# A mixture-of-experts tail on one Trainium2 core: token rows gathered per expert tile in place of rows scattered into a sorted buffer

## The reference

```python
x = x + attention(layernorm(x), context)
xn = layernorm(x)
probs = softmax(xn @ gate_w.T)
p, idx = top_k(probs, 2)
y_k = gelu(xn @ w1[idx_k].T + b1[idx_k]) @ w2[idx_k].T + b2[idx_k]      # k = 0, 1
out = x + sum over k of p_k * y_k
```

## Time and profile before

| | |
|---|---|
| median of 3 executions | 332.87 us (332.79 to 333.19) |
| profiled execution | 333.22 us |
| its span (first to last record) | 331.5 us |
| PE busy | 258.6 us |
| ACT busy | 231.7 us |
| DVE busy | 172.8 us |
| POOL busy | 79.4 us |
| mean granted clock of PE | 0.925 of 2.4 GHz |

### The profile page before, as it was taken

The page is one execution under the profiler, slowest core; times in us unless marked ns, Lnnn a source line. Parts: engine busy times, 40 slices in busy tenths (PEclk is TensorE's granted clock), DMA queues, the critical chain, the costliest instruction groups (busy, mean ns, idle before and its releaser), DMA issues.

```text
span 331.5 us, 6252 instructions
## 1 busy us (share of the span) xinstructions
PE 258.6 (78%) x1856; PEld 126.5 (38%) x1856; DVE 172.8 (52%) x422; ACT 231.7 (70%) x365; POOL 79.4 (24%) x134
## 2 busy tenths in 40 slices
PE   2689687399999999989899999986474079999940
PEld 2455445112222121212122222225463069898940
DVE  4798944224454535353545354447751327676612
ACT  4358565379999999999999999971794025555520
POOL 8893002100000000000000000402057604444430
PEclk9999965879999999999999999999898559999995
DMA  7999580010101010101010010199501171001114
GB/s 199 373 397 405 191 176 2 17 29 2 36 4 40 0 40 12 28 12 28 16 24 22 18 28 11 36 356 272 70 26 55 48 185 34 31 28 33 34 32 190
DMA packets 28930, 29.29 MB, mean 88 GB/s; under 512 B 15261, under 2 KB 22833, under 8 KB 28784
## 3 DMA queue, kind: packets, MB, share of 16 engines
q1 hardware_dynamic: 27456, 26.21, 26.4%
q0 software_dynamic: 1456, 2.86, 2.9%
HBM read 21.62 MB, written 7.45 MB: 88 GB/s over the span
## 4 chain that ended last, share of the span: by engine, by line
issue 31%; PE 23%; ACT 16%; DVE 11%; POOL 6%; SPq 5%; DMA 4%; ACTq 1%; DVEq 1%; POOLq 1%
ACT w2T L996 8%; ACT arenaB L996 8%; PE bank L1280 7%; PE bank L1401 5%; PE bank L1262 5%; SPq L318 4%; PE bank L1409 3%; POOL qS L380 3%; DVE arenaC L528 2%; DVE arenaB L899 2%; SPq L290 1%; PE bank L1170 1%; DMA arenaA<-ys_dram 1%; DMA x_sb<-in_x_dram 1%; DVE arenaB L905 1%
## 5 line engine op out<-in xcount | busy, mean ns | idle before, releaser
L716 DVE TENSOR_TENSOR arenaA<-bank,arenaA 128x512 f32<-128x512 f32 x80 | 55.2, 690 | 82.7 <-PE bank L1280 82.7
L996 ACT ACTIVATE arenaB<-bank 128x1024 f32<-128x1024 f32 x80 | 77.5, 1022 | 8.5 <-PE bank L1262 6.5
L996 ACT ACTIVATE w2T<-bank 128x1024 f32<-128x1024 f32 x80 | 76.7, 1028 | 3.0 <-PE bank L1262 1.7
L1262 PE MATMUL bank<-qS,keys 64*128 64x512 bf16 x324 | 63.4, 393 | 13.9 <-ACT w2T L996 5.7
L1262 PEld LDWEIGHTS bank<-qS,keys 64*128 64x128 bf16 x324 | 15.3, 93 | 101.9 <-ACT w2T L996 50.1
L1026 ACT ACTIVATE mask_u<-bank,arenaB 128x128 f32<-128x128 f32 x92 | 26.3, 369 | 39.2 <-PE bank L1401 39.2
L1280 PE MATMUL bank<-arenaB,vcur 128*32 128x512 f32 x320 | 44.4, 627 | 1.1
L1280 PE MATMUL bank<-w2T,vcur 128*32 128x512 f32 x320 | 42.6, 605 | 0.0
L402 POOL CAST keep<-flags 128x1 f32 x11 | 2.1, 189 | 142.9 <-DVE arenaC L628 142.1
L472 POOL DMA_INDIRECT ys_dram<-arenaB,mask_u x23 | 22.3, 969 | 35.0 <-DVE arenaB L905 35.0
L1401 PE MATMUL bank<-arenaB 128*128 128x128 f32 x184 | 27.2, 295 | 2.3 <-DVE arenaB L891 2.3
(11 more groups left out here) (300 smaller groups left out, 321.5 us busy)
## 6 DMA issues: line engine op xcount, KB each, us to landing
mask_u<-in_L_ffn_w_dram SPq DMA_DIRECT2D x2, 2048.0 KB, 10.4
mask_u<-in_mask_BxSxS_bk_dram SPq DMA_DIRECT2D x6, 560.5 KB, 12.6
ctx_sb<-in_ctx_dram SPq DMA_DIRECT2D x3, 768.0 KB, 12.9
qS<-qparts_dram SPq DMA_DIRECT2D x4, 448.0 KB
mask_u<-in_mask_BxSxS_bk_dram SPq DMA_DIRECT2D x6, 240.0 KB, 10.8
keys_in<-kparts_dram SPq DMA_DIRECT2D x40, 32.0 KB
mask_u<-in_mask_BxSxS_bk_dram SPq DMA_DIRECT2D x1, 1121.0 KB, 8.2
xs_dram<-w1T SPq DMA_DIRECT2D x2, 520.0 KB, 18.0
```

The source lines that it names most:

```text
L716: nc.vector.tensor_tensor(a, bank[:, 4 + k % 2, :], a, ALU.add).then_inc(s["ac"], 1)
L996: nc.scalar.activation(probs[u % 8], bank[:, 2 * (u % 2):2 * (u % 2) + 2, :].rearrange("p a b -> p (a b)"), ACT.Exp, scale=SCALE).then_inc ...
L1262: last = mm(bank[:, 2 * (u % 2) + a, :], keys[rows, g, :], qS[rows, g, cols], start=not hides, stop=True, tile_position=(64 * a, 0))
```

## The change

The buffer `xs_dram`, its fill and the 16 scatters are gone. ACT writes all normalised rows once (8 instructions, now ahead of its exp and of the weight turns), and SP writes them to `xn_dram`. DVE compares each pair's slot with all 128 places of a tile (`in_tile`, bf16, 128x1024 for each choice) and with all 23 tiles (`hot_tile`). PE multiplies these by the token's number in two parts (`by_tile`), in 24 short bf16 products between weight turn 3 and weight turn 4. DVE reads from the sums, for each slot, the row to gather (`x_row`) and the row to write (`y_row`). POOL gathers a tile's 128 rows with one indirect DMA each: six ahead of the tile loop, then one after each of the first 17 scatters. The gates are no longer applied in the loop, where DVE only copies; they are applied at the end, in 16 instructions that multiply and add. DVE now evicts weight turns 12 to 15, and the products with b2 move from ahead of the tile loop into it.

The core of the diff:

```diff
-            sp.wait_ge(s["fill"], 2)
-            for b in range(3):
-                sp.dma_start(xs_dram.rearrange("(j s) c -> s j c", s=P)[:, b:NT:3, :],
-                             fill[:, b:b + 1, :].broadcast_to([P, len(range(b, NT, 3)), ROW])).then_inc(s["xs_fill"], 16)
-            sp.wait_ge(s["scat"], 16 * 2 * QT)
-            for k, (j0, j1) in enumerate(XS_CUTS):
-                sp.dma_start(xs_sb[:, j0:j1, :], ...).then_inc(xs_in[k], 16)
+            sp.wait_ge(s["cq_sb"], 2 + QT)
+            sp.dma_start(xn_dram.rearrange("(p t) d -> p t d", t=QT), xn2).then_inc(s["xn_out"], 16)
...
-            nc.gpsimd.memset(fill[:, :, :], 0.0).then_inc(s["fill"], 1)
-            pool.wait_ge(s["fill"], 1)
-            nc.gpsimd.iota(fill[:, :, ROW - 1].bitcast(I32), ...).then_inc(s["fill"], 1)
...
-            for k in range(2):
-                for t in range(QT):
-                    nc.gpsimd.indirect_dma_start(xs_dram, ..., rows[k][:, t, :], None).then_inc(s["scat"], 16)
+            def gather(j):
+                nc.gpsimd.indirect_dma_start(xs_sb[:, j, :], None, xn_dram, ...x_row[:, j:j + 1]...).then_inc(xs_in[j % AHEAD], 16)
+            pool.wait_ge(s["xn_out"], 16)
+            pool.wait_ge(s["map_sb"], 2)
+            for j in range(AHEAD):
+                gather(j)
             for j in range(NT):
-                pool.wait_ge(s["yacc"], j + 2)
+                pool.wait_ge(s["yacc"], j + 1)
                 nc.gpsimd.indirect_dma_start(ys_dram, ...)
+                if j + AHEAD < NT:
+                    pool.wait_ge(xs_in[j % AHEAD], 16 * (j // AHEAD + 1))
+                    gather(j + AHEAD)
...
             # DVE, after slots
+            map_step(nc.vector.tensor_scalar(tile_i, slots, 7, None, ALU.logical_shift_right), 1)
+            map_step(nc.vector.tensor_copy(tile_f, tile_i), 2)
+            map_step(nc.vector.scalar_tensor_tensor(within, tile_f, -float(P), slots_f, ALU.mult, ALU.add), 3)
+            nc.vector.tensor_tensor(in_tile[:, 0:QT, :], cc(within, P)[:, 0:QT, :], iota_q..., ALU.is_equal)
+            map_step(nc.vector.tensor_tensor(hot_tile, cc(tile_f, NT), iota_j..., ALU.is_equal), 4)
+            nc.vector.tensor_scalar(by_tile[:, :, 0, :], hot_tile, pcol, None, ALU.mult)
+            nc.vector.tensor_tensor(by_tile[:, :, 1, :], hot_tile, cc(ccol, NT), ALU.mult).then_inc(s["map_in"], 1)
+            nc.vector.tensor_tensor(in_tile[:, QT:2 * QT, :], ..., ALU.is_equal).then_inc(s["map_in"], 1)
...
-                nc.vector.tensor_scalar(ysb[:, j % 3, :], bank[:, 4 + j % 2, 0:P], xs_sb[:, j, D:D + 1], None, ALU.mult).then_inc(s["yacc"], 1)
+                nc.vector.tensor_copy(ysb[:, j % 3, :], bank[:, 4 + j % 2, 0:P]).then_inc(s["yacc"], 1)
...
-                nc.vector.tensor_tensor(x2, x2, back[k]..., ALU.add).then_inc(s["fin"], 1)
+                for t in range(QT):
+                    nc.vector.scalar_tensor_tensor(x2[:, t, :], back[k][:, t * D:(t + 1) * D], gates[:, k, t:t + 1], x2[:, t, :], ALU.mult, ALU.add).then_inc(s["fin"], 1)
...
             # ACT: the eight rows ahead of exp, then only twelve weight turns
+            act.wait_ge(s["sqrt2"], 7)
+            for t in range(QT):
+                nc.scalar.activation(xn2[:, t, :], x2[:, t, :], ACT.Identity, scale=..., bias=...).then_inc(s["cq_sb"], 1)
             nc.scalar.preload_act_table(ACT.Exp)
-            for k in range(16):
+            for k in range(ACT_TURNS):
```

More of the change, by code:

```diff
@@ L227, in build @@
         mask_in = [[None] + [sem(f"mask_in{b}_{t}") for t in range(1, QT)] for b in range(len(MASK_CUTS))]
[L228 removed]
+        xs_in = [sem(f"xs_in{k}") for k in range(AHEAD)]
         y_out = [sem(f"y_out{k}") for k in range(3)]
@@ new lines, in _ @@
+            dve.wait_ge(s["map_ps"], 1)
+            part, column, second = (bank[:, 2, k * NT:k * NT + NT] for k in range(3))
+            raw, full, goal = (row_f[:, k, 0:NT] for k in range(3))
+            nc.vector.tensor_scalar(full, part, float(QT), None, ALU.mult).then_inc(s["map_sb"], 1)
+            dve.wait_ge(s["map_sb"], 1)
+            nc.vector.tensor_tensor(raw, full, column, ALU.add).then_inc(s["map_at"], 1)
+            dve.wait_ge(s["map_at"], 1)
+            nc.vector.tensor_scalar(x_row, raw, -float(QT), 0.0, ALU.add, ALU.max).then_inc(s["map_sb"], 1)
@@ new lines, in _ @@
+            nc.vector.scalar_tensor_tensor(goal, second, float(S), raw, ALU.mult, ALU.add).then_inc(s["map_sb"], 1)
+            nc.vector.scalar_tensor_tensor(full, full, 0.0, spare, ALU.is_equal, ALU.mult).then_inc(s["map_at"], 1)
+            dve.wait_ge(s["map_sb"], 3)
+            nc.vector.tensor_scalar(goal, goal, -float(QT), 0.0, ALU.add, ALU.max).then_inc(s["map_sb"], 1)
+            dve.wait_ge(s["map_at"], 2)
+            dve.wait_ge(s["map_sb"], 4)
+            nc.vector.tensor_tensor(y_row, goal, full, ALU.add).then_inc(s["map_sb"], 1)
@@ L914, in _ @@
                     slot_rows(j + 2)
-                gated(j)
+                result(j)
+                if j == 2:
+                    for k in range(2):
+                        dve.wait_ge(s["gT_ps"], k + 1)
+                        nc.vector.tensor_copy(epi_e[:, 512 * k:512 * k + 512], bank[0:E, 6 + k, :]).then_inc(s["gT_sb"], 1)
+                if j == 5:
+                    dve.wait_ge(s["b2ps"], 1)
+                    nc.vector.tensor_tensor(x2, x2, bank[:, 6:8, :].rearrange("p a (t d) -> p (a t) d", d=D), ALU.add).then_inc(s["b2ps"], 1)
+            dve.wait_ge(s["b2ps"], 2)
             for k in range(2):
@@ L1388, in slots_turn, with b2_products @@
+            def b2_products():
+                pe.wait_ge(s["b2_in"], 32)
+                pe.wait_ge(s["gT_sb"], 2)
+                for t in range(QT):
+                    last = mm(bank[:, 6 + t // 4, (t % 4) * P:(t % 4 + 1) * P], epi_e[:, t * P:(t + 1) * P], b2_sb[:, :], start=True, stop=True)
+                last.then_inc(s["b2ps"], 1)
             def slots_turn(j):
-                if j in first:
-                    pe.wait_ge(xs_in[first[j]], 16)
+                pe.wait_ge(xs_in[j % AHEAD], 16 * (j // AHEAD + 1))
```

162 lines of the change are left out of this document (93 added, 69 removed).

## The result

| kernel | median of executions | profiled execution | its span |
|---|---|---|---|
| before | 332.83 us (331.48 to 333.19, four) | 333.22 us | 331.5 us |
| changed | 340.13 us (336.56 to 340.56, four) | 340.13 us | 338.4 us |

The ratio is 1.0179, with a 95% interval from 1.0135 to 1.0223: slower by 1.8%, where 330.0 and a gain of 0.9% were forecast, in a range that ended at 334.0. The experiments add a second half to this result: on two further chips the changed kernel is slower too (ratios 1.024 and 1.038), and on one it is faster, at 0.989 (0.984 to 0.994).

A forecast was written before the change was run, and what follows sets the result against it. The bound was taken as the stretch of scatters, read-back and cold start ahead of the loop, then PE and DVE in it. Terms -0.6 - 10.5 + 5.6 - 0.8 + 1.0 + 1.0 + 1.4 = -2.9 gave 330.0 us, range 326.8 to 334.0.

The forecast's parts named there:

- F: Tile loop: POOL becomes the bound with 40 DMAs instead of 23; 27 pitches at 1.29 us, +1.0 us.
- C: Tile loop: gates' transposes, b2 products, DVE copies and an addition moved in, +5.6 us; 3.0 if DVE's part lies beside PE's.
- D: Tile loop: the result is copied at 0.277 in place of 0.346 us, on the path every second tile, -0.8 us.
- E: Tile loop: 17 gathers hold up DVE's copies by 0.23 us for half of them, +1.0 us, bounds 0 and 3.9.
- A: At 54 to 58 us: POOL's fill instructions leave the chain, -0.6 us.
- B: Ahead of the loop: without the scatters the loop starts earlier, third tile's `up` at 262.3 against 272.77 us, -10.5 us.
- G: End of kernel: 16 multiply-adds for the gates replace two additions, +1.4 us, between +0.9 and +2.9.
- Rival 1: Loop: POOL's 40 DMAs run at 1.42 us or more rather than 1.29; 333.6 us at 1.42; chance 0.19.
- point of decision of 1.40: POOL's DMA pitch in us at which the forecast median passes "no change" from before.
- POOL idle for less than 0.4 between scatter 6 and 22: Sign in the loop that POOL's queue is the bound: no POOL pause of 0.4 us or more at a time.
- Rival 3: Loop: each of 17 gathers holds up a copy for 0.96 instead of 0.23 us, +6.2, 336.2 us; chance 0.05.
- Rival 4: Loop start: tile 0's rows come after the weights; 333.0 us with 3 us beyond the 5 spare; chance 0.03.

The follow-up runs named there:

- Chip 5: Changed kernel run again unmodified, beside three variants: 329.62 us, ratio 0.989 to before, loop 52.7 us, no stalls.
- chips 1, 4 and 6: Changed kernel, unmodified, on the first result's chip and in two later sets: 340.13, 344.64 and 342.00 us; the loop stalls on all three.
- chip 3: Set without stalls, changed kernel not run: its variants with loop gathers unread or replaced took 326.76 to 329.28 us; before with 17 gathers added, 338.88.
- chip 2: Set of four variants of the changed kernel, itself not run there; without the loop's 17 gathers 327.05 us, the others 339.06 to 342.14.
- all gathers first: Changed kernel with all 23 gathers issued ahead of the first scatter and eight result buffers: 325.98 us on one chip, 347.61 on another.
- late rows: Reading of the changed kernel with loop gathers issued but not read (329.13 us, later 345.60): TensorE waits for a gather's landing.

## Why the prediction was wrong

**The sign.** The forecast was 330.0. Chip 5 gave 329.62 and chips 1, 4 and 6 gave 340.1 to 344.6. The step that failed is *F*: it priced POOL's second DMA per tile by the time that POOL needs for it, 27 pitches, +1.0 us, and held DVE's and PE's waits on the queue to be all that could come of it. On chips 1, 4 and 6 the signals between engines that have nothing to do with these DMAs also come late beside them, 2.6 us at a time on chip 1, and the loop took 61.9 to 65.8 us in place of 53. No term stood for that.

The trace of before shows it once, in a stretch that the prediction took only for its DMA pitches. While the 16 row scatters follow each other without a pause, PE hands the products with b2 (L1382) to DVE's addition L883, which waits for nothing else:

```profile
252.32 2.05 PE L1382 MATMUL bank<-b_sb,ctx_sb 8*128 8x128 f32 x16 [1.60 <-DVE ctx_sb L880]
...
258.01 1.22 DVE L883 TENSOR_TENSOR ctx_sb<-ctx_sb,bank 128x1024 f32<-128x1024 f32 x1 [5.75 <-remote]
```

The products are over at 254.37 and the addition starts at 258.01, 3.6 us later, with no releaser in the trace: the same sign as in the loop above. The kernel before with gathers added has the same two instructions beside the same 16 scatters. On chip 3:

```profile
252.35 2.05 PE L1392 MATMUL bank<-b_sb,ctx_sb 8*128 8x128 f32 x16 [0.93 <-DVE ctx_sb L890]
...
254.44 1.22 DVE L893 TENSOR_TENSOR ctx_sb<-ctx_sb,bank 128x1024 f32<-128x1024 f32 x1 [2.14 <-PE bank L1392]
```

There it starts 0.04 us after the products, and 0.03 us after them on chip 5. So the late signal does not need the changed kernel, nor gathers. Before, it lay under the scatters and cost nothing; the change put handovers of every tile where it could be paid.

Term by term, on chip 5, where the sum can be checked (last scatter at 315.96, forecast 319.80 - 4.3 = 315.5). C, D, E and F together are 52.7 - 46.2 = 6.5 us there, forecast 6.8; how they share it is taken from other chips:

- **A, -0.6: -0.5 at its place.** From the start of POOL's cast (L394 before, L404 after) to the next load it took 57.84 - 54.53 = 3.31 us before and 57.91 - 55.10 = 2.81 on chip 5 (58.04 - 55.24 = 2.80 on chip 1). In these executions all that stands ahead of the cast was 0.6 to 0.7 us later than in the trace of before, so no later start shows the gain.
- **B, -10.5: right, partly by luck.** The third `up` starts at 262.01 there and at 261.69 on chip 1, forecast 261.7 with A. The map's products start at 245.59 on chip 5, forecast 245.7, and at 246.54 on chip 1, where routing was 1 us later. They take 1.0 us on chip 5 where 2.1 was priced, though the granted clock was 0.50 as assumed; the weights behind them take 8.9 in place of 8.2, and the two misses nearly cancel.
- **C, +5.6: too large.** The loop without gathers (chip 2) took 2.5 us more than before's, C and D together, so C is about 3.3 by D's own price. The lower value given, 3.0 (DVE's part beside PE's), was nearer.
- **D, -0.8: nearly as said,** L959 takes 290 ns against 346 for L905, 0.06 us each rather than 0.07; on how many tiles it was on the path isn't shown.
- **E, +1.0: nothing, for a reason that the rows show.** The weight copies L953 take 439 ns in the mean on chip 5 and 477 on chip 1, and the same copies (L899) took 550 before; the copies ahead of them (L951) take 445 and 458, against 433 for L897:

```profile
L899 DVE COPY arenaB<-w2T 128x512 f32 x23 | 12.6, 550 | 0.0
L953 DVE COPY arenaB<-w2T 128x512 f32 x23 | 11.0, 477 | 0.1
L953 DVE COPY arenaB<-w2T 128x512 f32 x23 | 10.1, 439 | 0.1
```

  (Before, chip 1, chip 5.) Of the 46 copies of both lines 17 take 0.5 us or more in the trace of before, 12 on chip 1 and 5 on chip 5. Every one of the 34 starts 0.53 to 0.68 us after the start of an indirect DMA and ends 1.18 to 1.22 us after it, as the 0.65 us at 278.40 beside the scatter from 277.87 do. One that starts 0.9 us after it takes 0.42 (283.03 and 282.13), and only two that start within those 0.15 us stay short. So a copy is held up by where it falls in a DMA, not by how many DMAs there are; E multiplied a price by a number of DMAs.
- **F, +1.0: on chip 5 right in kind, too small.** From scatter 6 to scatter 17 POOL never rests: 279.11 to 308.52 is 29.41 us for 22 pitches, 1.337 each, not 1.29. From scatter 6 to 22 it takes 36.85 us where before took 33.27: +3.6.
- **G, +1.4: +1.8.** The last scatter to the end of the span is 13.5 us, against 11.7. The 16 records take 0.344 us each, overlapped to 0.274, and each group of eight pays its own tail:

```profile
321.98 2.19 DVE L986 SCALAR_TENSOR_TENSOR ctx_sb<-arenaA,ctx_sb 128x128 f32<-128x128 f32 x8 [6.30 <-DMA arenaA<-ys_dram]
324.27 2.19 DVE L986 SCALAR_TENSOR_TENSOR ctx_sb<-ctx_sb 128x128 f32<-128x128 f32 x8
```

C was some 2.3 too high and F 2.6 too low, so that 329.62 lies next to 330.0 on chip 5 is in part luck.

**The rivals.** Rival 1 had the sign of the first result, but not its mechanism: the pitch was 1.34 on chip 5, below its point of decision of 1.40, and on chip 1 POOL waited where the time was lost. "POOL idle for less than 0.4 between scatter 6 and 22" held on chip 5 until scatter 20 and failed on chip 1, with 1.6 us at every third tile. Rival 3's rule (the Trainium skill, SBUF — State Buffer, "Who interferes with whom") would have made 336.2 by DVE copies that wait for a whole instruction. No copy took more than 0.65 us, and taken together they did not get longer on either kind of chip, so the rule's price was not paid here. Rival 4 did not come about: the rows were there before the weights.

**What stays open.** Why chips (or occasions) differ, and whether the time is lost in an execution that nobody records. Every execution timed here was recorded: each has its span and clock. In the traces of the stalling chips many signals are missing (the views name "remote" in place of a releaser, and give no landing time for the gathers), and in those of chips 3 and 5 they are there. The trace of before lacks them too: no landing time for its scatters, where the same scatters land in 2.3 and 2.4 us in the median on chip 3. The kernel without gathers in the loop lacks some as well and does not stall. The Trainium skill (NOTIFIC — the notification-queue block, "Overflow: three behaviours, one of which stalls the engine") says that the path on which such records leave can, when its queue is full, drop new records or stall their producer. That would fit both signs, and no run here shows it. It wasn't tried on a chip that stalls: the kernel before with gathers added, the fill or the second scatter in a gather's place, and a pause between the indirect DMAs. Nor was one of the chips 2 to 6 used a second time.

## What to carry to other kernels

Price an indirect DMA on POOL at its pitch (1.26 us alone, 1.34 in a loop beside DVE), and ask separately what a queue of them without a pause does to engines that hand each other work meanwhile. Look in the trace for a handover beside such a queue, even where it costs nothing yet: compare the releaser's end with the start behind it, and take a wait with no releaser in the trace as a sign; if there is no such stretch, give it a bound of its own. Before two variants are compared, run both on one chip: here the chip was worth 15 us for the same program, and a clean reading of a single set ("late rows") was wrong. A version that wins on a quick chip, like all gathers first, has to be run on the other kind as well; of the two orders that ran on both kinds here, neither beats the kernel before on both.

## What was not expected of the hardware

- The same program takes 329.6 us on one chip and 340.1, 344.6 and 342.0 on three other occasions, while a program with one indirect DMA per tile stays within 332.6 to 334.9 on all.
- On a stalling chip DVE acts 18.2 us late on a transpose that PE had finished by its records, while gathers are issued every 1.25 us, and engines go on 3.06 us after the start of the last. The kernel before has one such handover 3.6 us late, hidden under its scatters.
- The stalls of the changed kernel come at a period of 9.2 us, with three or six result buffers and with six or eleven gathers ahead.
- A DVE copy of 128x512 words that starts 0.53 to 0.68 us after the start of an indirect DMA is held until 1.18 to 1.22 us after it; one that starts outside of that takes 0.40 to 0.47 us. With 17 more DMAs in the loop there were fewer held copies, not more (12 and 5 of 46 against 17).
